# A two-layer transformer kernel: mask by multiplication, input statistics moved to the feed-forward, whole-state products, five states weighed by GpSimd, statistics by ScalarE

## What is computed

```python
def _layernorm(x, eps=1e-05):
    return (x - x.mean(-1)) / sqrt(x.var(-1) + eps)

# layer 0: causal attention, 16 heads of 16, ALiBi bias; then a gated MLP with FP4 quantised operands
x = x + ga * attention(_layernorm(x) * (1 + ca) + sa)
x = x + gb * fp4_mlp(_layernorm(x) * (1 + cb) + sb)
# layer 1: a selective state space, 512 channels (Dn) x 16 states (n)
h = _layernorm(x) * (1 + ca) + sa          # "h1" in the kernel
xn = _layernorm(h) * ln_w + ln_b           # the second norm of this part
x_inner, z = split(xn @ W_in.T);  u = silu(conv4(x_inner))
dt = clip(softplus(dt_low @ W_dt.T + b_dt) + 0.001, 0.001, 0.1)
hs = exp(dt * A[n]) * hs + (dt * u) * B[n]   # a scan over the tokens, for each state n
y = sum over n of hs * C[n];  y = (y + u * D) * silu(z)
x = x + ga * (y @ W_out.T + h)
# then a mixture of low-rank experts, 2 of 6
```

## Time and profile before

| | us |
|---|---|
| three runs | 4206.35, 4210.48, 4210.94; median 4210.48 |
| the profiled execution | 4207.32, span 4205.4 |
| granted TensorE clock, mean over the span | 0.881 |
| busy: PE, DVE, ACT, POOL | 3374.6, 3592.4, 2249.4, 2620.3 |

### The profile page before, as it was taken

How to read it: one execution, slowest core, us unless ns; L and a number is a source line. 1 busy time by engine, 2 the same in 40 slices (tenths; PEclk the granted TensorE clock), 3 DMA queues, 4 the chain that set the end, 5 groups by cost and what they waited for, 6 DMA issues and landing times. The chain is left out here.

```text
span 4205.4 us, 60689 instructions
## 1 busy us (share of the span) xinstructions
PE 3374.6 (80%) x21452; PEld 1522.8 (36%) x21452; DVE 3592.4 (85%) x6348; ACT 2249.4 (53%) x3974; POOL 2620.3 (62%) x2515
## 2 busy tenths in 40 slices
PE   5979999999994999999567777777777777777467
PEld 3623333333332555565222222222222222222166
DVE  5768888888855999999289999999999999999966
ACT  5626666666672333333265665666665565665422
POOL 1102322222222888887188888988889898988823
PEclk8969999999996999999778887888888888887689
DMA  4884565656513111110112222222222222212122
GB/s 146 279 175 67 75 88 67 88 75 82 77 32 87 35 44 47 47 43 26 47 48 52 69 59 62 67 58 50 54 69 60 66 65 56 67 51 52 40 93 83
DMA packets 273931, 299.55 MB, mean 71 GB/s; under 512 B 34559, under 2 KB 204662, under 8 KB 273622
## 3 DMA queue, kind: packets, MB, share of 16 engines
q1 hardware_dynamic: 273630, 295.68, 31.7%
HBM read 210.22 MB, written 84.51 MB: 70 GB/s over the span
## 5 line engine op out<-in xcount | busy, mean ns | idle before, releaser
L1679 POOL TENSOR_TENSOR d_dBu<-d_dtu,d_Bn 128x1024 f32<-128x1024 f32 x512 | 1202.7, 2377 | 157.7 <-DVE d_h L1746 157.5
L1525 ACT ACTIVATE d_dA<-d_dt,d_decay 128x512 f32<-128x512 f32 x1024 | 688.6, 687 | 414.2 <-DVE d_h L1746 412.5
L745 ACT ACTIVATE b_P<-b_pT 128x512 f32<-128x512 f32 (+1 forms) x1120 | 571.4, 576 | 328.8 <-PE b_pT L653 328.5
L1746 DVE TENSOR_TENSOR_SCAN d_h<-d_dA,d_last_h,d_dBu 128x512 f32<-128x512 f32 x512 | 616.9, 1265 | 21.2 <-ACT d_dA L1525 18.2
L1746 DVE TENSOR_TENSOR_SCAN d_h<-d_dA,d_dBu 128x512 f32<-128x512 f32 x512 | 587.1, 1205 | 50.3 <-ACT d_dA L1525 47.9
L775 DVE CUSTOM_DVE_ANT_0 b_pS<-b_pS,mask_qk 128x512 f32<-128x512 f32 (+3 forms) x1024 | 581.2, 618 | 50.1 <-PE b_pS L663 45.1
L663 PE MATMUL b_pS<-KS,QS 99*128 99x512 bf16 (+3 forms) x1536 | 471.4, 339 | 71.7 <-DVE b_Gc L775 47.3
L625 POOL TENSOR_SCALAR_AFFINE_SELECT b_P<-b_P 128x128 f32<-128x128 f32 (+2 forms) x608 | 191.4, 321 | 506.1 <-ACT b_P L745 493.3
L653 PE MATMUL b_pT<-QS,KS 118*128 118x512 bf16 (+3 forms) x1536 | 450.1, 330 | 19.5 <-ACT b_gT L729 16.3
L1753 DVE TENSOR_TENSOR d_h<-d_h,d_C 128x2048 f32<-128x2048 f32 x192 | 434.6, 2263 | 0.5 <-PE d_C L1408 0.5
L1408 PE MATMUL d_C<-d_bc,d_pick 96*128 96x512 bf16 x256 | 118.0, 461 | 359.5 <-DVE d_h L1753 359.2
(11 more groups left out here) (300 smaller groups left out, 5906.5 us busy)
## 6 DMA issues: line engine op xcount, KB each, us to landing
d_Bn<-scratch_bs SPq DMA_DIRECT2D x64, 1024.0 KB, 8.2
scratch_parts<-a_part SPq DMA_DIRECT2D x48, 512.0 KB, 4.1
...
scratch_v<-a_v SPq DMA_DIRECT2D x16, 1024.0 KB, 7.6
...
```

The lines of the kernel that those rows point to most:

```text
L745: act.activation(t[:, heads[0]:heads[-1] + 1, c * CH:c * CH + w], pT[:, place % RING, 0:len(heads) * w].rearrange("p (h w) -> p h w", w=w) ...
L1525: act.activation(dA[:, m % 2, :], dt[:, c.k % 2, m, :], ACT.Exp, scale=decay[:, m, n:n + 1]).then_inc(dA_d, 1)
L1679: pool.tensor_tensor(dBu[:, n % 2, 2 * j:2 * j + 2, :], dtu[:, c.k % 2, 2 * j:2 * j + 2, :], Bn[:, n // BG % 2, n % BG, :].unsqueeze(1).to ...
L1746: dve.tensor_tensor_scan(h[:, n % HS, m, :], dA[:, m % 2, :], dBu[:, n % 2, m, :], start, ALU.mult, ALU.add).then_inc(scanned, 1)
```

## The change

Attention: the mask is no longer a select by position. A table cap holds integer 1 on and below the diagonal and 0 above it, and GpSimd multiplies the 32-bit patterns of the exponentials by it. The fill value of the table that hides later keys (edge) goes from -1e30 to -1024.

Feed-forward: two ages more (s_ and v_, lags 10 and 11). ScalarE adds up the finished row x2 with an accumulating copy, scales the sum, and adds up the squares of its deviations with an accumulating Square, into two tables of 128x64 that stay in SBUF.

State space: GpSimd makes reciprocal deviations and biases of all 64 tiles at once at the start (four instructions on 128x64, one of them a power). The statistics of x go away, and those of h1 go from VectorE to ScalarE (total_of under 7, variance under 9). The products are whole states, 128x2048, in three buffers; B comes two states a load. POOL_C becomes (0, 3, 6, 9, 12). normalise of h1 moves to 12 and 13, scale_bias to 11. In SyncE's block the sem_inc that followed waits (wait_before) is left out.

```diff
@@ attend, drop_masked
-                pool.affine_select(out=own, in_=own, compare_op=ALU.is_ge, fill=0.0,
-                                   base=0, pattern=[[0, len(heads)], [-1, P]], channel_multiplier=1).then_inc(p_masked, 1)
+                pool.tensor_tensor(own.bitcast(I32), own.bitcast(I32), K["cap"][:, :].unsqueeze(1).to_broadcast([P, len(heads), P]), ALU.mult).then_inc(p_masked, 1)
@@ feed_forward, scalar engine
+                if v_ is not None:
+                    n = v_.base * U + v_.k
+                    wait(act, sum_d, v_.times(1, 1))
+                    act.activation(K["x2_neg"][:, n:n + 1], x2_sum[:, n % 2, :], ACT.Copy, scale=-1.0 / (16.0 * D)).then_inc(neg_d, 1)
...
+                if v_ is not None:
+                    n = v_.base * U + v_.k
+                    wait(act, neg_d, v_.times(1, 1))
+                    act.activation(unread[:, n % 2, :], x[:, n % XS, :], ACT.Square, bias=K["x2_neg"][:, n:n + 1], scale=1.0 / 16.0, accum_out=K["x2_var"][:, n:n + 1]).then_inc(var_d, 1)
+                if s_ is not None:
+                    n = s_.base * U + s_.k
+                    wait(act, x2_d, s_.times(1, 1))
+                    wait(act, var_d, s_.times(1, -1))
+                    act.activation(unread[:, n % 2, :], x[:, n % XS, :], ACT.Copy, accum_out=x2_sum[:, n % 2, :]).then_inc(sum_d, 1)
@@ constants
-POOL_C = (0, 4, 8, 12)
+POOL_C = (0, 3, 6, 9, 12)
-HS, BG = 4, 4
+HS, BG, BS = 4, 2, 3
@@ state_space, scalar engine
+            def total_of(f, tiles):
+                if 0 in tiles:
+                    wait(act, h_mul, f.times(1, 1))
+                    wait(act, h1_d, f.times(1, 1))
+                    wait(act, xn2, f.times(1))
+                for t in tiles:
+                    last = act.activation(x[:, t, :], h1[:, t, :], ACT.Copy, accum_out=st[:, t:t + 1])
+                if CT - 1 in tiles:
+                    last.then_inc(stat, 1)
+                    wait(act, stat, f.times(2, 1))
+                    wait(act, rs, f.times(1))
+                    act.activation(mv[:, 0, :], st[:, :], ACT.Copy, scale=-1.0 / (16.0 * D)).then_inc(neg_d, 1)
+
+            def variance(f, tiles):
+                if 0 in tiles:
+                    wait(act, neg_d, f.times(1, 1))
+                for t in tiles:
+                    last = act.activation(x[:, t, :], h1[:, t, :], ACT.Square, bias=mv[:, 0, t:t + 1], scale=1.0 / 16.0, accum_out=mv[:, 1, t:t + 1])
+                if CT - 1 in tiles:
+                    last.then_inc(stat, 1)
...
-                 {4: lambda f: normalise(f, 0, (2, 3)), 10: lambda f: normalise(f, 1, (1,)), 12: lambda f: normalise(f, 1, (3,)), 15: lambda f: turned(f, 1)}),
+                 {4: lambda f: normalise(f, 0, (2, 3)), 7: lambda f: total_of(f, (0, 1)), 9: lambda f: variance(f, (0, 1)), 12: lambda f: normalise(f, 1, (0, 1)), 13: lambda f: normalise(f, 1, (3,)), 15: lambda f: turned(f, 1)}),
...
-                 {3: lambda f: normalise(f, 0, (0, 1)), 9: lambda f: normalise(f, 1, (0,)), 11: lambda f: normalise(f, 1, (2,)),
+                 {3: lambda f: normalise(f, 0, (0, 1)), 7: lambda f: total_of(f, (2, 3)), 9: lambda f: variance(f, (2, 3)), 12: lambda f: normalise(f, 1, (2,)),
@@ state_space, gpsimd
-                    wait(pool, b_in[g % 2], c.times(32, 16 * (g // 2) + 16))
-                for j in range(2):
-                    wait(pool, scanned, c.times(NS * MD, MD * (n - 2) + 2 * j + 2))
-                    pool.tensor_tensor(dBu[:, n % 2, 2 * j:2 * j + 2, :], dtu[:, c.k % 2, 2 * j:2 * j + 2, :],
-                                       Bn[:, n // BG % 2, n % BG, :].unsqueeze(1).to_broadcast([P, 2, CH]), ALU.mult).then_inc(dBu_d, 1)
+                    wait(pool, b_in[g % 2], c.times(8 * NS // BG, 16 * (g // 2) + 16))
+                wait(pool, scanned, c.times(NS * MD, MD * (n + 1 - BS)))
+                pool.tensor_tensor(product(c, n), dtu[:, c.k % 2, :, :], Bn[:, n // BG % 2, n % BG, :].unsqueeze(1).to_broadcast([P, MD, CH]), ALU.mult).then_inc(dBu_d, 1)
...
+            pool.tensor_tensor(rstd_x[:, :], K["x2_var"][:, :], eps[:, :], ALU.add).then_inc(sx_step, 1)
+            pool.tensor_tensor(nmr_x[:, :], K["x2_neg"][:, :], sixteen[:, :], ALU.mult).then_inc(sx_step, 1)
+            pool.wait_ge(sx_step, 2)
+            pool.tensor_tensor(rstd_x[:, :], rstd_x[:, :], half[:, :], ALU.pow).then_inc(sx_step, 1)
+            pool.wait_ge(sx_step, 3)
+            pool.tensor_tensor(nmr_x[:, :], nmr_x[:, :], rstd_x[:, :], ALU.mult).then_inc(sx, 1)
...
-                ({15: finish}, {14: step_input}, {3: lambda f: scale_bias(f, 0), 6: shift, 8: lambda f: scale_bias(f, 1)}))
+                ({15: finish}, {14: step_input}, {6: shift, 11: scale_bias}))
@@ state_space, vector
+                wait(dve, dBu_d, c.times(NS, n + 1))
                 for m in range(MD):
-                    if m % 2 == 0:
-                        wait(dve, dBu_d, c.times(2 * NS, 2 * n + m // 2 + 1))
                     wait(dve, dA_d, c.times(NS * MD, MD * n + m + 1))
                     start = 0.0 if c.k % 2 == 0 else last_h[:, n, m, :]
-                    dve.tensor_tensor_scan(h[:, n % HS, m, :], dA[:, m % 2, :], dBu[:, n % 2, m, :], start, ALU.mult, ALU.add).then_inc(scanned, 1)
+                    dve.tensor_tensor_scan(h[:, n % HS, m, :], dA[:, m % 2, :], product(c, n)[:, m, :], start, ALU.mult, ALU.add).then_inc(scanned, 1)
 
...
-            def stats(f, j):
-                if j == 0:
-                    wait(dve, x_in, f.times(16, 16))
-                else:
-                    wait(dve, h1_d, f.times(1, 1))
-                src = x if j == 0 else h1
-                wait(dve, stat, f.times(4, 2 * j))
-                for t in range(CT):
-                    last = dve.bn_stats(st[:, t, :], src[:, t, :])
-                last.then_inc(stat, 1)
-                wait(dve, stat, f.times(4, 2 * j + 1))
-                wait_before(dve, rs, f.times(2, j - 1), passed)
-                for t in range(CT):
-                    last = dve.bn_aggr(mv[:, j, t, :], st[:, t, :])
-                last.then_inc(stat, 1)
...
-                 {1: lambda f: stats(f, 0), 4: modulate, 6: lambda f: stats(f, 1), 13: carry}))
+                 {4: modulate, 13: carry}))
```

More of the change, by code:

```diff
@@ L31 @@
 MASKED = -1.0e30
+BELOW = -1024.0
+CAP = 1
 EPS = 1e-5
@@ L1038, in _, with step @@
             pe.wait_ge(w_in, 16)
-            def step(a, e, n_, d, b, h_, q, c, o_):
+            def step(a, e, n_, d, b, h_, q, c, o_, s_, v_):
                 if a is not None:
```

112 lines of the change are left out of this document (65 added, 47 removed).

## The result

The changed kernel takes 4261.06 us, median of 4 runs (4256.65 to 4262.3), against 4208.73 (4206.35 to 4210.94) before: the ratio is 1.0121, with a 95% interval of 1.0108 to 1.0134. It is slower, as forecast, and the forecast of 4260 is 1 us off. The profiled execution has a span of 4260.6, 55.2 more than before.

| part | landmark | forecast | measured |
|---|---|---|---|
| attention | end of its last transposes, 1269.5 to 1292.3 | +23 | +22.8 |
| weights and feed-forward | last x2, 2016.6 to 2040.9 | +0.5 | +1.5 |
| start of state space | first gate_y, 2248.5 to 2284.7 | +10.5 | +11.9 |
| steady chunks | first to 14th gate_y, 1531.9 to 1547.7 | +18.2 (13 of +1.4) | +15.7 |
| last two chunks | to the 16th gate_y | -1.5 | +0.7 |

What follows compares the result with a forecast made beforehand. TensorE bounds attention, VectorE feed-forward and state space, but other engines' waits return its savings. Chunks +20, last two -1.5, start +10.5, feed-forward +0.5, attention +23: +52.5 on 4207.3, 4260 us; range 4205 to 4295.

Steps and rivals of the forecast that it cites:

- the float rate: Attention mask: the integer product costs 2.19 ns an element, 1.26 us at 512, so TensorE waits, +23 us.
- Rivals 2 and 3: Respectively: mask costs as the select, chunk -1.1, 4202 to 4215, chance 0.08; integer product slow, +90, 4327, chance 0.05.
- Start: State-space start: GpSimd's 64-column power, 10.4 us, precedes the first normalisation; first h1 statistics slower on ScalarE; together +10.5 us.
- (a): State 3: removed x statistics are given back, as VectorE waits for a decay behind TensorE's convolution; 1.4 us a chunk.
- small waits: Steady chunk: half of the first product and a decay behind TensorE's projection no longer cost waits; -0.8 us.
- (b): Removed h1 statistics lay under ScalarE's Silu block, so VectorE's scan starts no earlier; all 1.8 us a chunk given back.
- (c): ScalarE's accumulating activations for h1, taken as 0.55 us each, make VectorE wait at states 7 and 8; 1.0 a chunk.
- (d): GpSimd's moved states leave no weighing before states 5, 8, 11; waits at 4 and 11 cost 1.7 us a chunk.
- (e): Whole product 15, queued behind weighing and dtu on GpSimd, lands later, so VectorE waits; cost 2.1 us a chunk.
- rival 4: GpSimd becomes the bound, so the change takes nothing off the path; inside the range, chance 0.04.
- what should show it: VectorE idle 14 us a chunk, weighings 176, no BATCH_NORM; wrong if chunks are under 114 us, among other signs.
- Rival 1: Faster: VectorE is the bound and work leaving it is gained, -85 us, with start and mask 4156; chance 0.13.

Runs made afterwards that it cites:

- experiment 1: The change with the select of before as mask again, in place of the integer product: 4241.38 us, ratio 1.0075 to the kernel before.
- experiment 4: The change with GpSimd's power split, 4 columns first and 60 behind the first chunk's scaled bias: 4247.09 us, ratio 1.0093 to the kernel before.
- experiment 5: The change with the four statistics of x and aggregates on VectorE again behind gate_y, results unread: 4264.92 us, ratio 1.0124 to the kernel before.
- experiment 7: The change with ScalarE taking convolution tiles 0, 1, 2 after the first two decays of states 3, 4, 5: 4243.5 us, ratio 1.0072 to the kernel before.
- experiment 3: The change with h1's statistics on VectorE again at state 6, scaled bias at 8, normalisations at 9 to 12: 4282.59 us, ratio 1.0170 to the kernel before.
- experiment 6: The change with GpSimd weighing four states, 0, 4, 8, 12, so VectorE weighs one more: 4264.31 us, ratio 1.0122 to the kernel before.

## Why the prediction was right, and where it was not

The mechanism is right: what leaves VectorE was no gain, since other engines end its waits at just those places. That the total comes within 1 us is luck, since terms inside miss by 0.6 to 1.2 us a chunk and cancel.

- **Attention: right.** 1.27 us for the block of four heads against 1.26 from the float rate, +22.8 against +23; experiment 1 takes it back alone. Between 128 and 512 elements the product takes (1270 - 455)/384 = 2.12 ns an element. The rule of the Trainium skill (GPSIMD Engine Reference, Engine selection) that the ordinary elementwise path computes in fp32 fits this time; the time alone does not show which path the product took. The prediction's estimate by the rate in the Trainium skill was 1.11 and a dispatch. Rivals 2 and 3 fell with the 1.27.
- **Start: right in cause, 1.4 short.** The power takes 10.56 against 10.4, and experiment 4 removes it. From the end of shift (2072.5) to h1's scaled bias (2078.5) it is 6.0, forecast 6.7.
- **Feed-forward and end: missed by a little.** The feed-forward is +1.5 against +0.5. The last two chunks and the rest are +3.3 against -1.5; no run followed them.
- **(a) x statistics: right in cause, under-sized.** Forecast 1.4 at state 3, measured 2.67 and, in odd chunks, 2.48; experiment 5 shows the cover, experiment 7 what ends the wait. The -0.8 booked under small waits came at state 0 (0.85 before, none now); in addition gate_y waits 2.0 in place of 2.9. What the forecast left out is TensorE's clock behind gate_y. Three chunks of the change, 6.7 us each from 1.9 us after gate_y, then the first eight matmuls of their convolutions:

```profile
2880.40:2887.10 6.70, 6.14 (x37) 2.17 (x38) 6.70 (x6) 1.38 (x2) 6.70 (x2) 0.50 0.39 81
2523.73:2530.43 6.70, 6.16 (x40) 2.36 (x40) 6.70 (x6) 1.38 (x2) 6.70 (x3) 0.75 0.29 78
3477.83:3484.53 6.70, 4.79 (x40) 1.71 (x40) 6.70 (x6) 2.71 (x5) 6.70 (x3) 1.00 0.33 78
2882.91 5.79 PE L1520 MATMUL d_f<-d_xi,d_cdiag 128*128 128x512 f32 x8
2525.35 5.37 PE L1520 MATMUL d_f<-d_xi,d_cdiag 128*128 128x512 f32 x8
3479.46 3.70 PE L1520 MATMUL d_f<-d_xi,d_cdiag 128*128 128x512 f32 x8
```

  At 1.2 GHz throughout (0.50) state 3 waits 2.67, at 1.2 GHz for half of it (0.75) 1.15, at 2.4 GHz (1.00) not at all. The kernel before has the middle case in every chunk, and wherever the change has it the wait is 1.15 to 1.41, the forecast's 1.4.
- **(b) h1 statistics under the Silu block: right.** 2.57 (odd chunks 2.76) against 2.95; in experiment 3 VectorE's waits fall by about what they take.
- **(c) Accumulating activations: over-sized.** 0.40 and 0.49 against 0.55, the copy below my lower bound of 0.5. Of the two waits one is 0.17, the other absent; 0.2 against 1.0. As I read it, I had taken the rate of a normalisation with its own bias and scale for a plain copy.
- **(d) Missing weighings: half right.** 0.42 at state 4 (forecast 0.6). State 11 waits 1.91, and the 1.39 of states 9 and 10 are gone: +0.5 against +1.1. What I missed is 1.8 us at states 13 and 14 in even chunks (0.2 before), 0.4 in odd ones. With GpSimd's states at every third place, TensorE sums state 9 at state 12, between two tiles of the gate projection and ahead of C:

```profile
2954.23 3.75 PE L1511 MATMUL d_f<-d_xnT,w_inT 128*128 128x512 f32 x4
2957.91 2.79 PE L1456 MATMUL d_y<-d_h,d_eye 32*32 32x512 f32 x64
2960.62 1.99 PE L1511 MATMUL d_f<-d_xnT,w_inT 128*128 128x512 f32 x4
2962.45 0.38 PE L1439 MATMUL d_C<-d_bc,d_pick 96*128 96x512 bf16 x1
```

  Two sums where there was one (x32) put C of state 12 and two tiles of the gate 1.65 us later, and decays stand behind both on ScalarE. In experiment 6, without it, the wait at 13 is gone; experiment 3, which left the sum there, kept it. The sums are not the whole cause: they stand in every chunk, and in four of the change's thirteen state 13 waits 0.03 at most. TensorE's stretches at 1.2 GHz fall elsewhere in those; the share of each stays open.
- **(e) Product 15: right.** 2.30 and 2.23 against 2.1. Not foreseen was its other side: a whole product can hold VectorE inside its short instructions. The prediction did not price it, and in the change that comes out about even (1.78, 1.06, 0.72 and 0.34 for the modulation, the two splits and the carry of half the chunks against 1.47, 1.45, 0.82 and 0.12: 3.90 and 3.86 a chunk). It was luck of position.
- **Sum of a chunk: +1.2 over thirteen and +1.5 in the eight, against +1.4.** In the eight, VectorE's work is 5.1 less (forecast 5.75) and its waits 6.6 more (7.2). GpSimd 848.7/8 = 106.1 us busy a chunk (105.5), not the bound; rival 4 is out. Of what should show it, weighings are 176 and no batch statistics are left; the chunk is 119.3.
- Rival 1 fell by experiments 5 and 6: 1.75 and 2.26 us of VectorE's work put back in a chunk, one apart from the other, left the total as it was and cost 0.4 and 0.7 us a chunk between the 1st and 14th gate_y.
